# Two-layer graph network on one core: neighbour weights added into the stored adjacency by indirect DMAs, in place of rows gathered from a table

## The reference

```
h  = relu(layernorm(x))
# layer 0
d  = 1 / sqrt(rowsum(adj))
z  = leaky_relu((d * (adj @ (d * h))) @ W1 + b1, 0.1)
S  = exp(-sqrt(max(|z_i|^2 + |z_j|^2 - 2 z_i.z_j, 0) + 1e-10) / 2)   # 4096 x 4096
S  = S where it is among the 4 largest of its row, else 0
A2 = S + adj
d2 = 1 / sqrt(rowsum(A2))
x  = x + (d2 * (A2 @ (d2 * h))) @ W2 + b2
# layer 1
h2 = relu(layernorm(x))
x  = x + h2 @ W_self.T + (adj @ h2) @ W_neigh.T + b
```

## Time and profile before

| what | value |
|---|---|
| median of 3 runs | 1305.23 us (1304.32 to 1310.51) |
| the profiled execution's own time | 1303.21 us |
| its span in the trace | 1301.2 us |
| mean granted TensorE clock over the span | 0.886 |
| busy: TensorE / VectorE / ScalarE / GpSimd | 934.7 / 888.0 / 597.3 / 657.8 us |
| moved by DMA | 357.73 MB, mean 275 GB/s |

### The profile page before, as it was taken

The page is one execution under the profiler, slowest core; times in us unless marked ns, Lnnn a source line. Parts: engine busy times, 40 slices in busy tenths (PEclk is TensorE's granted clock), DMA queues, the critical chain, the costliest instruction groups (busy, mean ns, idle before and its releaser), DMA issues.

```text
span 1301.2 us, 13552 instructions
## 1 busy us (share of the span) xinstructions
PE 934.7 (72%) x3570; PEld 664.9 (51%) x3570; DVE 888.0 (68%) x852; ACT 597.3 (46%) x1105; POOL 657.8 (51%) x936
## 2 busy tenths in 40 slices
PE   0132154474776999899999994666777777799998
PEld 0111022232333444477777773455666666588886
DVE  1966665654554321288999999937777777788885
ACT  0533343162460322255555555635555554567673
POOL 9798779877820000044444444588888887200000
PEclk9985676786987999899999998788888888899999
DMA  9999999999996975295444445695777777599993
GB/s 222 323 349 367 363 343 382 349 365 351 354 374 230 357 266 187 92 262 200 158 157 157 155 157 206 184 379 203 282 279 271 284 274 273 215 358 384 381 382 124
DMA packets 117253, 357.73 MB, mean 275 GB/s; under 512 B 34528, under 2 KB 59872, under 8 KB 89568
## 3 DMA queue, kind: packets, MB, share of 16 engines
q1 hardware_dynamic: 60896, 273.11, 55.2%
q0 software_dynamic: 47104, 80.00, 20.6%
q10 hardware_dynamic: 9216, 4.20, 1.2%
HBM read 250.02 MB, written 106.95 MB: 274 GB/s over the span
## 4 chain that ended last, share of the span: by engine, by line
PE 31%; POOL 21%; DMA 18%; issue 14%; DVE 11%; ACT 2%; SPq 1%; POOLq 0%; DVEq 0%; ACTq 0%
DMA araw<-in_adj_dram 15%; POOL zt_lo L576 11%; PE ps L1157 7%; POOL araw L365 7%; PE ps L1274 4%; PE ps L1275 4%; PE ps L1276 4%; PE ps L1252 2%; PE ps L1253 2%; PE ps L1254 2%; PE ps L1255 2%; DVE m L988 2%; DVE bmax L975 2%; DVE i L990 2%; POOL t_st L505 1%
## 5 line engine op out<-in xcount | busy, mean ns | idle before, releaser
L365 POOL DMA_DIRECT2D araw<-in_adj_dram x512 | 301.1, 597 | 66.4 <-ACTq L637 26.9
L1018 DVE TENSOR_TENSOR araw_r<-araw,tr_r 128x2048 fp32r<-128x2048 f32 x128 | 289.4, 2296 | 44.6 <-ACT tr_r L731 44.4
L731 ACT ACTIVATE tr_r<-araw 128x2048 fp32r<-128x2048 f32 x128 | 241.7, 1911 | 66.2 <-PE ps L1276 37.9
L576 POOL DMA_INDIRECT zt_lo<-neighbour_table,idx_st x128 | 193.9, 1515 | 45.7 <-issue 39.2
L714 ACT ACTIVATE araw<-ps,nsq 128x1024 f32<-128x1024 f32 x128 | 142.5, 1117 | 115.3 <-PE ps L1255 96.0
L1274 PE MATMUL ps<-araw_r,zt_hi 128*128 128x512 f32 x256 | 110.2, 430 | 93.2 <-DVE araw_r L1018 63.9
L633 ACT ACTIVATE ps<-araw 128x256 f32<-128x256 f32 x304 | 111.1, 365 | 59.4 <-DMA araw<-in_adj_dram 55.3
L886 DVE TENSOR_REDUCE part<-araw 128x16 f32<-128x4096 f32 x13 | 57.4, 4413 | 98.1 <-DMA araw<-in_adj_dram 98.1
L1252 PE MATMUL ps<-sq_rows,pick 128*128 128x512 f32 x256 | 102.3, 400 | 17.7 <-POOL zs_lo L493 10.8
L1274 PE MATMUL ps<-araw_r,ys_r 128*128 128x512 f32 x256 | 101.7, 397 | 9.5 <-DVE araw_r L1018 9.5
L1274 PEld LDWEIGHTS ps<-araw_r,zt_hi 128*128 128x128 f32 x256 | 52.1, 204 | 109.5 <-DVE araw_r L1018 69.4
(11 more groups left out here) (150 smaller groups left out, 1654.7 us busy)
## 6 DMA issues: line engine op xcount, KB each, us to landing
araw<-transposed SPq DMA_DIRECT2D x152, 1024.0 KB, 6.2
araw<-in_adj_dram POOLq DMA_DIRECT2D x512, 128.0 KB, 21.2
keys_scratch<-araw SPq DMA_DIRECT2D x64, 512.0 KB, 4.2
transposed<-tr SPq DMA_DIRECT2D x28, 1024.0 KB, 9.0
transposed<-unit_zt_hi SPq DMA_DIRECT2D x18, 1024.0 KB, 8.7
transposed<-unit_zt_lo SPq DMA_DIRECT2D x18, 1024.0 KB, 9.4
xs<-in_x_dram SPq DMA_DIRECT2D x64, 64.0 KB, 2.1
araw<-transposed SPq DMA_DIRECT2D x8, 512.0 KB, 7.4
```

Of the source, the lines that this page charges most:

```text
L365: gp.dma_start(araw[R * q + first:R * q + R:SPREAD, c], adj_v[q, first:R:SPREAD, g // 2, g % 2, :, c]).then_inc(a_first_in[c], DMA)
L576: gp.indirect_dma_start(out=gath[:, i, u, k, :], out_offset=None, in_=table, in_offset=bass.IndirectOffsetOnAxis(ap=idx_st[:, i, u * TOPK ...
L731: act.activation(ring_hi[:, place % TSLOTS], ring[:, j], ACT.Copy).then_inc(hi_done, 1)
L1018: v.tensor_tensor(ring_lo[:, j], ring[:, j], ring_hi[:, place % TSLOTS].bitcast(F32), ALU.subtract).then_inc(lo_done, 1)
```

## The change

The neighbours' part of the second pass no longer comes from a table. Each of the 4 weights of each row is added to its cell in the DRAM array `transposed` before the second pass reads it, and subtracted again before the third pass reads it. Each is an indirect DMA with `compute_op=ALU.add` of 128 elements of 4 bytes (one for each partition), 16 for each group of 512 rows: 128 additions (`merge`) and 128 subtractions (`restore`).

- Gone: `h @ W2` in the first pass and its stores, the table and its store, the 128 gathers, the 16 weighted additions of a group on VectorE (`finish_second_a` keeps the residual's 4), and the extra transposition of the diagonal unit.
- New on GpSimd: `find_cells` (14 small instructions a group) works out the cells. From the fifth pair of the search on, 3 additions are issued in each pair (36 of the 128); the other 92 are issued after the last pair, and all 128 subtractions behind them.
- New waits: SyncE waits for `merged[g]` before the loads of group g of the second pass, and for `restored[g]` before those of the third. `restore(g)` waits until the second pass has used the group (`u_used`).
- Moved: weights, `d2` and the two parts of `ys` are made group by group within the search (`distance_part`, `second_degree`, `second_inverse` and `second_y_low` on VectorE, `neighbour_weights`, `second_root` and `second_y_high` on ScalarE). The candidates of a pair are searched one pair later, between the next pair's block maxima and its odd tile. `h2`'s high part goes to ScalarE, its low part and the bias b2 to VectorE, and the bias b to TensorE (4 matmuls a group with one row of ones).
- The loops of GpSimd, ScalarE, VectorE and SyncE are written out. Columns of the distances stand in another order, so that a cell's address follows from its place. The first pass has 10 buffers for transposed units where it had 7, and a load above the diagonal waits only for its own unit's store, where all of them waited for all stores.

```diff
@@ sync
-            for i in range(UT):
-                sp.wait_ge(at_out[i], STORED[i])
...
-            sp.wait_ge(gw_ready, 1)
-            for q in range(QD):
-                sp.dma_start(table_v[q], hs[R * q:R * q + R]).then_inc(table_out, DMA)
...
+            for pair in range(PAIRS):
+                keys_store(pair)
+                if pair == PAIRS - 4:
+                    sp.wait_ge(t_used, USED1)
+                    sp.wait_ge(merged[0], MERGE)
+                    for j in range(GROUPS // 2):
+                        load_unit(0, j)
...
+            for g in range(1, GROUPS):
+                sp.wait_ge(merged[g], MERGE)
+                for j in range(GROUPS):
+                    load_unit(g, j)
+            for g in range(GROUPS):
+                sp.wait_ge(restored[g], MERGE)
+                for j in range(GROUPS):
+                    load_unit(GROUPS + g, j)
@@ gpsimd
+            def add_cells(g, i, k, done):
+                gp.indirect_dma_start(
+                    out=at_cells, out_offset=bass.IndirectOffsetOnAxis(ap=idx[:, g * U + i, k:k + 1], axis=0),
+                    in_=vals[:, g * U + i, k:k + 1], in_offset=None,
+                    bounds_check=N * N - 1, compute_op=ALU.add).then_inc(done[g], DMA)
...
+            def restore(g):
+
+                gp.wait_ge(u_used, (g + 1) * GROUPS)
+                gp.wait_ge(merged[g], MERGE)
+                gp.wait_ge(deg2, g + 1)
+                gp.tensor_scalar(vals[:, U * g:U * g + U], vals[:, U * g:U * g + U], -1.0, None, ALU.mult).then_inc(neg_ready, 1)
+                gp.wait_ge(neg_ready, g + 1)
+                for i in range(U):
+                    for k in range(TOPK):
+                        add_cells(g, i, k, restored)
...
+            for pair in range(PAIRS):
+                if pair >= 1:
+                    keep_top(pair - 1, 1)
+                if 2 * pair + 3 < TILES:
+                    stage_tile(2 * pair + 3)
+                if pair >= 4:
+                    merge(into, into + 2)
+                    into += 2
+                if pair >= 1:
+                    keep_top(pair - 1, 0)
+                keep_blocks(pair)
+                read_blocks(pair)
...
+                if pair >= 4:
+                    merge(into, into + 1)
+                    into += 1
...
+            find_cells(GROUPS - 1)
+            merge(into, TILES * TOPK)
+            for g in range(GROUPS):
+                restore(g)
@@ vector
+            for pair in range(PAIRS):
+                search_blocks(pair)
+                if pair >= 1:
+                    search_candidates(pair - 1)
+                search(pair)
+                if pair >= 2 and pair % 2 == 0:
+                    distance_part((pair - 2) // 2)
+                if pair >= 4 and pair % 2 == 0:
+                    second_inverse((pair - 4) // 2)
+                if pair >= 3 and pair % 2:
+                    second_degree((pair - 3) // 2)
+                if pair >= 5 and pair % 2:
+                    second_y_low((pair - 5) // 2)
```

More of the change, by code:

```diff
@@ L299, in gnn_kernel @@
-        for g in reversed(range(GROUPS - 1)):
-            for c in range((g + 1) // 2, CHUNKS):
-                for half in range(CHUNK_UNITS):
-                    own = c == g // 2
-                    units_b.append((g, c, half, range(half * U + own, half * U + U, 1 + own)))
-        assert len(units_b) % GROUPS == 0
-        B_IN = len(units_b) // GROUPS * DMA
-        USED1 = TILES_A + sum(len(u[-1]) for u in units_b)
+        units_a = [(g, j) for g in range(GROUPS) for j in range(GROUPS)]
@@ new lines, in gnn_kernel, with late_diag @@
+        LATE = [U <= g < GROUPS - 1 for g in range(GROUPS)]
+        def late_diag(g, j):
+            return g >= 0 and LATE[g] and j == 0
+        used_after = [None] * len(units_a)
+        TILES_A = 0
+        for n, (g, j) in enumerate(units_a):
+            due = [n] if j < g else []
+            if late_diag(g - 1, j):
+                due.append((g - 1) * GROUPS + g - 1)
+            if j == GROUPS - 1 and not LATE[g]:
+                due.append(g * GROUPS + g)
+            for m in due:
+                TILES_A += U
+                used_after[m] = TILES_A
@@ L307, in gnn_kernel @@
+        STORED = [sum(n % UT == i for n in range(len(units_a))) * DMA for i in range(UT)]
+        units_b = [(g, j) for g in reversed(range(GROUPS - 1)) for j in range(g + 1, GROUPS)]
+        B_IN = [sum(n % GROUPS == i for n in range(len(units_b))) * DMA for i in range(GROUPS)]
+        USED1 = TILES_A + len(units_b) * U
         F1 = [GROUPS - 1] + list(reversed(range(GROUPS - 1)))
@@ L310, in gnn_kernel @@
         CAND = TOPK * DMA
-        GATHER = U * TOPK * DMA
+        MERGE = U * TOPK * DMA
+        PAIRS = TILES // 2
         STORE = QD * DMA
@@ L339, in gnn_kernel @@
         SPLIT_SQ = [t + 2 + LAG for t in STAGE_C]
-        LATE = [U <= g < GROUPS - 1 for g in range(GROUPS)]
-        def late_diag(g, c, half):
-            return g >= 0 and LATE[g] and c == 0 and half == 0
         def wait_alone(eng, signal, value):
@@ L592, in _ @@
-            hi_g, lo_g = [h.rearrange("p (u g) f -> p g u f", g=GROUPS) for h in (h_hi, h_lo)]
-            gp.wait_ge(table_out, QD * DMA)
-            gp.wait_ge(top_kept, 2 * TILES)
-            for i in range(2):
-                gather_group(i, i)
-            gp.wait_ge(bias_in, 3 * DMA)
-            gp.wait_ge(y_lo_done, GROUPS)
-            with gp.Fori(1, GROUPS // 2) as pair:
-                for i in range(2):
-                    keep_h2(pair * 2 + (i - 2))
-                    gather_group(pair * 2 + i, i)
@@ L842, in _ @@
             v.memset(neghalf[:], -0.5).then_inc(const_st, 1)
+            v.memset(tiny[:], 1e-10)
+            for n in range(TILES):
+                v.memset(own_cell[:, n:n + 1], float(n // U * N * GI + n % U * R))
             link(v.memset(pick[:].bitcast(F32), 0.0))
@@ L918, in make_z @@
                 else:
-                    for p in range(2):
-                        v.wait_ge(z_out[p], GROUPS // 2 * QD * DMA)
                     v.wait_ge(bias_in, DMA)
@@ L1078, in finish_second_c @@
             def finish_second_c(g):
[L1080 to L1090 removed]
+                v.wait_ge(q_mm, g + GROUPS + 1)
```

812 lines of the change are left out of this document (351 added, 461 removed).

## The result

| | before | after |
|---|---|---|
| median | 1304.78 us (4 runs, 1301.27 to 1310.51) | 1403.05 us (4 runs, 1395.33 to 1407.08) |
| span of the profiled execution | 1301.2 us | 1405.3 us |
| mean granted clock | 0.886 | 0.852 |
| busy GpSimd | 657.8 us | 977.5 us |

The ratio is **1.0762** (95% interval 1.0722 to 1.0802): the changed kernel is 7.6% slower. The forecast was 1277 us, faster. The time is outside its likeliest case and just above the range's end, 1390. It is rival B, the addition that costs GpSimd more.

A forecast was written before the change was run, and what follows sets the result against it. GpSimd's in-order queue was to set the end: 809 + 5 + 288 + 121 + 10 = 1233 for the last subtraction, plus 40, a span of 1273 against 1301.2; 28 off the 1305.2 median gave 1277 us, range 1205 to 1390.

The forecast's parts named there:

- rival B: GpSimd's row behind the search: an addition costs more than a gather; at 1.5 us the kernel takes 1387 us; chance 0.22.
- The search so ends at 809: End of the search: 808.8, less 9 (first pass), plus 13 (VectorE's added work), less 4 (fewer waits for keys).
- `find_cells` of the last group (5 us): Start of GpSimd's row behind the search: working out the last group's cells takes 5 us.
- 220 x 1.31 = 288 us: GpSimd's row behind the search: 92 additions and 128 subtractions, each at a free gather's 1.01 us plus 0.30.
- 116 x 1.04 = 121 us: GpSimd's row behind the search: 116 of VectorE's 128 splits each hold it up by 1.04 us.
- 8 negations, 10 us: GpSimd's row behind the search: 8 negations with their waits, about 1.2 us each.
- Tail 40: From the last subtraction's issue to the span's end: landing, first unit, its parts, 96 matmuls and the close, 40 us.
- About 80 us saved ahead of the third pass: Stages before the third pass: about 80 us gained, with 60 to 65 lost again in the third pass.
- A: Second and third pass: splits don't hold up the additions and TensorE sets the pace, 1211 us; chance 0.15.
- C: Second and third pass: the DMA engines become the limit, 1375 us at 1.0 us an addition; chance 0.12.
- D: Search: new GpSimd and ScalarE work waits on each other, 2 us more a pair, 1309 us; chance 0.08.
- GpSimd with its `keep_h2` work fills: Second pass of the kernel before: GpSimd's gathers and `keep_h2` work fill the group's period of 34 us.

The follow-up runs named there:

- run 2: The changed kernel with its 256 indirect DMAs as plain scatters, without the add: 1312.81 us.
- run 6: The kernel before with the add switched on in its 128 gathers from the table: 1363.19 us.
- run 3: The changed kernel with the second input of VectorE's split taken from PSUM (wrong low parts): 1271.77 us.
- run 5: The changed kernel with three of the four neighbours added and subtracted, 192 indirect DMAs in place of 256: 1284.37 us.
- run 4: The changed kernel with its 128 subtractions sent to a spare DRAM array and no wait for them in the third pass: 1362.29 us.
- run 7: The kernel before with a row's own values read from SBUF, 12 gathers a group instead of 16: 1297.13 us, ratio 0.9966.
- run 8: The kernel before with the second input of VectorE's split taken from PSUM (wrong low parts): 1287.12 us.
- run 9: The kernel before with VectorE's finish of a second-pass group cut in two and moved forward: 1310.94 us, ratio 1.0065.
- run 10: The kernel before with own rows read from SBUF (12 gathers a group) and VectorE's finish cut in two and moved forward: 1289.54 us, ratio 0.9893.

## Why the prediction was wrong

Step by step, on the profiled execution (forecast against trace):

- **"The search so ends at 809": right.** The last FIND_INDEX8 starts at 809.78 and takes 0.69 us. The loads above the diagonal are issued 9.75 us earlier (402.36 for 412.11), and seven pairs in a row (674 to 787) took 15.3 to 17.4 us, 16.2 in the mean, where 16.3 was forecast.
- **"`find_cells` of the last group (5 us)": wrong, 18.5 us to the first addition.** I costed 14 short instructions as if GpSimd were alone, in a stretch where VectorE runs split after split, and held the indirect DMAs alone for sensitive to them. +13.5.
- **"220 x 1.31 = 288 us": wrong, and this is the step that decides.** The sum took the gather's 1.01 us "because the row's number of offsets is the same". It is 1.55 us, so 220 x 1.85 = 407: +119. Runs 2 and 6 put it down to the addition itself, and runs 2, 3 and 5 show that the kernel's end follows the row's.
- **"116 x 1.04 = 121 us": right.** The 220 behind the search have a mean of 2.098 us: 220 x (2.098 - 1.55) = 121. 113 splits ran beside them, 1.07 us each. Run 3 takes it away.
- **8 negations, 10 us**: about 6. They overlap the additions' ends.
- So the last subtraction comes at 1233 + 13.5 + 119 - 4, about 1362; the trace has it issued at 1361.98 and done at 1363.5. **Tail 40: right, 42** (the first loads are issued at 1364.97).
- **What I costed at nothing stayed at nothing**: the transpositions that went from the first pass, 12 instructions fewer a group on VectorE, TensorE's earlier start. Of its 13.5 us, 6 were left at the end of the second pass, and they were gone in the third.
- **"About 80 us saved ahead of the third pass": wrong.** TensorE began it at 1104.3, 6 us later than the 1098.7 of the kernel before, because the 92 additions held the second pass as well (280 us for 273; 217 in run 3). And "the third 184" read the window's border as the pass's start: TensorE took 196 us for it.

**Rivals.** *B* had the mechanism, its break-even (0.13 us) and a price, 1.5 us and 1387; measured were 1.55 us and 1403, the rest being, to a few us, the 0.05 us more on each of 220 (11 us) and `find_cells`. It had a chance of 0.22. The bounds of an unknown duration were 1.01 and 1.5, each with a reason from this kernel, and the sum needed it below 1.14: by its own bounds the forecast's side was the small part of the interval. That is where the odds should have come from, not from the closer likeness. The range's upper end was B's point value, without room for B's own doubt. *A* fell with the 3.3 us additions, and run 3 shows what is left without the hold-ups, 1272 us at 1.55 each. *C* fell with run 4. *D* fell: pairs took what was forecast. B's 1.5 us came near the measured 1.55, but from a count of accesses that no run here tests, so that closeness may be luck.

**The reading of the kernel before** was half right. "GpSimd with its `keep_h2` work fills" the 34 us is what the chain of waits shows. But busy 217.6 of 274 us and a lengthened gather do not show that a shorter row would shorten a group. VectorE waits for a gather only at the first group (18.68 us) and the last (3.70), and in between the second chain, of VectorE's finish and its splits, was as long. Runs 7 and 8 show that shortening GpSimd's row there gives 4 and 14 us, nearly all of it once, at the first group, and run 6 that lengthening it costs nearly its full price. So taking the gathers away could win little by itself, and the change put 220 longer DMAs there.

## What to carry to other kernels

Where a change makes one engine's in-order row the path, and the sum is that row's length times one duration that the trace does not show, take the chances from where break-even lies between the bounds, and try that duration alone first. An indirect DMA that adds is not the one that copies with a flag set. A full row on the chain of waits is a bound for what is added to it (run 6), but not for what is taken away, if a second chain of the same length lies beside it: moving one of the two gained 4 us (run 7) or lost 9 (run 9), moving both gained 12 (run 10). And a merge that must be undone is paid twice; here the additions alone gained about 15 us and the subtractions cost 114.

## What the runs showed of the hardware

- An indirect DMA over 128 offsets costs GpSimd 0.97 us for 4-byte numbers to DRAM and 1.01 for 512-byte rows to SBUF, and 1.54 to 1.55 us if it adds, with 0.30 before the next one. That the size of the pieces hardly matters was a surprise.
- VectorE's `tensor_tensor` over 2048 numbers a partition with both inputs in SBUF holds such DMAs up by 1.04 to 1.07 us on average (gathers and additions), and a GpSimd instruction of 0.2 us up to 2.17 us. With one input in PSUM it does neither (longest addition 1.81 us, longest instruction of `find_cells` 0.25 us; run 3), and takes as long itself.
- The reverse is there as well. In run 10 GpSimd's `tensor_tensor` additions over 512 numbers took 3.34 us instead of 1.29, and VectorE's splits 2.55 instead of 2.29 us on average.
- The DMA engines spend 0.02 us of all 16 on 128 plain four-byte writes (run 2), 0.20 on 128 rows of 512 bytes, 0.35 on 128 four-byte additions, and 0.56 on 128 rows that are added (run 6: 22.0% of 270 us for 107). So adding costs them about 0.35 us more in both cases.
